# Last convolution's output: GpSimd rounds image 0 in place, VectorE goes on with the sum of image 1

## The chip, the cores and the metric

The kernel runs on one core of one Trainium2 chip. The metric is the device time of one execution in microseconds, as the median of several runs. A core has TensorE (matmul, results in PSUM), VectorE, ScalarE and GpSimd for elementwise work, and SyncE, which here only starts transfers. The engines run side by side, each through its own list of instructions in order, and wait for one another by semaphores. GpSimd's work in this kernel reads and writes SBUF only.

## The reference, cut to what matters

The input is 4 images of 64 channels, 32 x 32 pixels. Four blocks follow each other: a spatial attention (L0), two 3x3 convolutions with quantised weights and batch norms (L1), two 3x3 convolutions with 4-bit weights and activations (L2), and a box convolution with batch norms (L3). The change is in the output of block L2:

```
def qfn(x, k):
    n = float(2 ** k - 1)
    return ste_round(x * n) / n

def act_quant(x, k):
    return qfn(jnp.clip(x, 0.0, 1.0), k)
...
out = act_quant(bn_eval(conv3x3(x, wq1), gamma1, beta1, mean1, var1), A_BIT)
wq2 = weight_quant(w2, W_BIT) * mask
out = bn_eval(conv3x3(out, wq2), gamma2, beta2, mean2, var2)
out = out + x
return act_quant(out, A_BIT)
```

Block L3 then takes this output in two ways: as the input of a 1x1 convolution to 16 channels (with a batch norm over all images and a relu), and as the residual of its own output.

## The kernel before

The kernel is written engine by engine: one Python function for each (`sp`, `pe`, `act`, `dve`, `pool`) lists its instructions in the order in which it runs them, with explicit waits (`wait_ge`) and signals (`then_inc`). No scheduler moves anything. All data stay in SBUF; an image is a tile of 128 partitions (64 channels, twice) by 512 elements.

The stage of the change is the end of L2. TensorE convolves the four images of the last convolution (`main_taps` and `side_taps3`, lines 476 and 507) into four PSUM banks, images 0 and 1 first, then 2, then 3. For each image VectorE's `outer(b)` adds the scaled convolution and `x15`, which is the block's input times 15 with the bias added, that GpSimd made earlier (L1328), into `tmpo` (the sum, L1119). It then adds a large constant, which rounds to an integer, and takes the minimum (L1122, in place in `tmpo`). ScalarE's `outer_clip(b)` subtracts the constant, clips at zero and writes the integers as bf16 into `xi` (ScalarE's lines all show as L685, its helper `run`). Image 3 has no clip on ScalarE: VectorE does it with two instructions (L1124, L1126), the second of which waits until ScalarE's clips of images 0 to 2 are signalled.

Within VectorE the helper `link` makes an instruction signal the semaphore `chain` and then waits for it, so that the next instruction finds the result written. The rounding therefore waits for the sum, while the sum of the next image doesn't wait for the rounding.

TensorE takes `xi` in this order: `spread(0)`, `spread(1)` (L614, for the residual), `bottleneck(0, 1, 2)` (L605, the 1x1 convolution of three images side by side in three groups of columns), `spread(2)`, `bottleneck(3)`, `spread(3)`. ScalarE copies each spread image from PSUM (`x_out`), after its three clips. VectorE, after image 3, transposes the first half of image 0's copy (`residual_out`, L1153) and takes the statistics of the bottleneck's result (`bn_stats` into `hst`, L1158), which waits for `bottleneck(3)`. From there single instructions on VectorE, TensorE and ScalarE make scale and shift, and the box convolution, the last batch norm, the relu and the stores follow. GpSimd does nothing between `x15` and the final sums (`pool_sums`, L1335 and L1337). Other lines that matter below: `add_residual` (L1103), the same form as the sum L1119, `low_part` (L903), VectorE's differences of `rows_w` (L1139) and GpSimd's clip of the edges (L1296).

Of the kernel before, what the change touches and what calls it, by code (L numbers as in the profile page):

```python
# [24 lines left out]
ALU = mybir.AluOpType  # L25
# [12 lines left out]
MAGIC = 12582912.0  # L38
QN, QP = -4.0, 3.0
LEVELS = 15.0  # L40
# [24 lines left out]
BANKS = ((6, 4, 5, 0), (7, 1, 2, 3))  # L65
# [25 lines left out]
def build(nc, x, wa, wg_raw, wconv, par, cst, out):  # L91
# [3 lines left out]
    for n, (kind, _) in enumerate(uses):  # L95
        by_act.append((by_act[-1] if by_act else 0) + (kind != "D"))
        by_dve.append((by_dve[-1] if by_dve else 0) + (kind == "D"))
# [3 lines left out]
    with ExitStack() as ctx:  # L101
        def sb(name, shape, dt=F32):
            return ctx.enter_context(nc.sbuf_tensor(name, [128] + shape, dt))

        def sem(name):
            return ctx.enter_context(nc.semaphore(name))
# [33 lines left out]
        ev_scale = sb("ev_scale", [2])  # L140
# [54 lines left out]
        tmpo = sb("tmpo", [NB, HALF])  # L195
        x15 = sb("x15", [NB, HALF])
# [7 lines left out]
        ps = ctx.enter_context(nc.psum_tensor("ps", [128, 8, 512], F32))  # L204
# [21 lines left out]
        def flat(t):  # L226
            return t.rearrange("q o n -> q (o n)")
# [23 lines left out]
        def split_count(k, b):  # L251
# [12 lines left out]
        sum_ready = sem("sum_ready")  # L264
        q_relu, q_int, q_ready = sem("q_relu"), sem("q_int"), sem("q_ready")
        x15_ready, xi_ready, xi_up = sem("x15_ready"), sem("xi_ready"), sem("xi_up")
        h_raw, h_stat, h_all, h_var, h_sqrt, h_ab, h_ready = (sem(n) for n in (
            "h_raw", "h_stat", "h_all", "h_var", "h_sqrt", "h_ab", "h_ready"))
        hblk_ready = sem("hblk_ready")
# [411 lines left out]
        def _(act):  # L681
            act.dma_start(wbc[:], wa[:, 0:256 + HEAD]).then_inc(wa_in, 16)

            def run(o, i, f, **kw):
                return nc.scalar.activation(o, i, f, **kw)  # L685
# [32 lines left out]
            for kind, i in uses:  # L718
                if kind != "S":
                    continue  # L720
                b, t = divmod(i, JT)
# [41 lines left out]

            def outer_clip(b):

                act.wait_ge(xi_up, b + 1)
                run(xi[:, b, :], tmpo[:, b, :], ACT.Relu, bias=consts[:, K_MAGIC:K_MAGIC + 1]).then_inc(xi_ready, 1)

            for b in range(NB):
# [3 lines left out]
            for b in range(NB - 1):  # L773
                outer_clip(b)
# [59 lines left out]
        def _(dve):  # L834
            V = nc.vector
            links = [0]

            def link(ins):

                links[0] += 1  # L840
                ins.then_inc(chain, 1)
                dve.wait_ge(chain, links[0])
# [155 lines left out]
            for kind, i in uses:  # L998
# [4 lines left out]
                b, t = divmod(i, JT)  # L1003
# [110 lines left out]
            def outer(b):  # L1114

                v = tmpo[:, b, :]
                dve.wait_ge(conv_done[3], b + 1)
                dve.wait_ge(x15_ready, b + 1)
                link(V.scalar_tensor_tensor(v, ps[:, BANKS[1][b], :], ev_scale[:, 1:2], x15[:, b, :],  # L1119
                                            ALU.mult, ALU.add))  # L1120
                if b < NB - 1:
                    V.tensor_scalar(v, v, MAGIC, MAGIC + LEVELS, ALU.add, ALU.min).then_inc(xi_up, 1)  # L1122
                    return
                link(V.tensor_scalar(xi[:, b, :], v, MAGIC, MAGIC, ALU.add, ALU.subtract))  # L1124
                dve.wait_ge(xi_ready, b)
                V.tensor_scalar(xi[:, b, :], xi[:, b, :], 0.0, LEVELS, ALU.max, ALU.min).then_inc(xi_ready, 1)  # L1126
# [17 lines left out]
            for b in range(NB):  # L1144
                outer(b)
# [114 lines left out]
        @block.gpsimd  # L1260
        def _(pool):
            G = nc.gpsimd
            links = [0]


            def link(ins):

                links[0] += 1
                ins.then_inc(pchain, 1)
                pool.wait_ge(pchain, links[0])  # L1270

            G.memset(wq[:].bitcast(F32), 0.0).then_inc(wq_zero, 1)
            G.memset(w2[:].bitcast(F32), 0.0).then_inc(wq_zero, 1)
            G.memset(w3[:], 0.0).then_inc(wq_zero, 1)
            pool.wait_ge(wq_zero, 3)
            pool.wait_ge(cst_in, 16)
            G.tensor_copy(ident_bf[:], consts[:, K_ID:K_ID + 128]).then_inc(id_ready, 1)
            pool.wait_ge(id_ready, 1)

            def pieces(t):  # L1280

                n = C * W // PIECES
                return [t[:, n * p:n * (p + 1)] for p in range(PIECES)]

            def edge(i, offset, table):


                n = C // PIECES
                for p in range(PIECES):
                    G.tensor_tensor(edge_buf[i][:, n * W * p:n * W * (p + 1)].rearrange("q (k j) -> q k j", j=W),  # L1290
                                    parm[:, offset + n * p:offset + n * (p + 1)].unsqueeze(2).to_broadcast([128, n, W]),
                                    consts[:, table:table + W].unsqueeze(1).to_broadcast([128, n, W]), ALU.add)\
                        .then_inc(edge_sum, 1)
                pool.wait_ge(edge_sum, PIECES * (i + 1))
                for v in pieces(edge_buf[i]):
                    G.tensor_scalar(v, v, 1.0, 0.0, ALU.min, ALU.max).then_inc(edge_clip, 1)  # L1296

            pool.wait_ge(par_in, 16)
            w1 = parm[:, P_W1:P_W1 + OC]
            link(G.memset(wp[:], 0.0))  # L1300
            link(G.tensor_copy(w1p[:, 0, :], w1))
            link(G.tensor_tensor(w1f[:], w1, w1p[:, 0, :], ALU.subtract))
            link(G.tensor_copy(w1p[:, 1, :], w1f[:]))
            link(G.tensor_tensor(w1p[:, 2, :], w1f[:], w1p[:, 1, :], ALU.subtract))
            link(G.tensor_copy(wp[0:64, :, 0:OC], w1p[0:64]))
            G.tensor_copy(wp[64:128, :, OC:2 * OC], w1p[64:128]).then_inc(wp_ready, 1)
            pool.wait_ge(wp_ready, 1)

            edge(0, P_XMAX, K_IR1)
            edge(1, P_XMIN, K_IR)  # L1310
            edge(2, P_YMAX, K_JW1)
            edge(3, P_YMIN, K_JW)

            pool.wait_ge(wmax_part, 2)
            G.partition_all_reduce(wmax_all[:], wmax[:], 128, bass.bass_isa.ReduceOp.max).then_inc(wmax_done, 1)
            pool.wait_ge(wmax_done, 1)
            G.memset(img3[:], 0.0).then_inc(img3_zero, 1)
            pool.wait_ge(img3_zero, 1)

            pool.wait_ge(lo_done, NB)  # L1320
            pool.wait_ge(edge_clip, 4 * PIECES)
            for hi, lo in zip(pieces(edge_buf[2]), pieces(edge_buf[3])):
                G.tensor_tensor(lo, hi, lo, ALU.subtract).then_inc(cols_ready, 1)  # L1323

            pool.wait_ge(ev_ready, 1)
            for b in range(NB):
                pool.wait_ge(gen[2], b + 1)
                G.tensor_scalar(x15[:, b, :], y3[:, b, :], LEVELS, ev_bias[:, 1:2], ALU.mult, ALU.add)\  # L1328
                    .then_inc(x15_ready, 1)

            def pool_sums(i):

                two = slice(SUM_POOL[2 * i], SUM_POOL[2 * i] + 2)
                pool.wait_ge(f_lin, 2 * i + 2)
                G.tensor_tensor(flat(fo[:, two, :]), flat(fo[:, two, :]), flat(xf[:, two, :]), ALU.add).then_inc(f_sum, 1)  # L1335
                pool.wait_ge(f_sum, i + 1)
                G.tensor_scalar(flat(fo[:, two, :]), flat(fo[:, two, :]), 0.0, None, ALU.max).then_inc(f_out_pool, 1)  # L1337

            pool.wait_ge(xf_ready, 2 * NB)
            for i in range(len(SUM_POOL) // 2):  # L1340
                pool_sums(i)
# [88 lines left out]
```

## Time and profile before

| what | value |
|---|---|
| median of 3 runs | 157.21 us (157.13 to 157.22) |
| the profiled execution | 158.21 us |
| its span | 156.4 us |
| TensorE matmul, busy share of the span | 90% |
| VectorE | 75% |
| ScalarE | 54% |
| GpSimd | 33% |
| mean granted TensorE clock | 0.98 |

The profiled execution is a run of its own: its time is 1.00 us above the median of the others, and 1.81 us of it lie outside the span. Busy shares are averages over stages with different limits. In rows of a timeline the first number is the start in us from the span's start, the second the time covered; "x3" with one time is three instructions that overlap or follow each other. A bracket tells how long the engine was idle before it and what ended that.

### The profile page before, as it was taken

To read this page: it belongs to the slowest core of one execution; us is meant where nothing else is said; L and a number is where in the kernel's file an instruction comes from. 1 tells how busy PE (TensorE), PEld (TensorE's weight loads), DVE (VectorE), ACT (ScalarE), POOL (GpSimd) and SP (SyncE) were. 2 spreads that over 40 slices of the span, in tenths; PEclk is the share of its full clock that TensorE was granted. 3 is DMA by queue.
4 is the path that set the end of the run, shared out by engine and by line. 5 is a ranking of instruction groups with operands and counts; after the bars stand their busy time and mean duration, and the time that the engine had idled before them with its cause. 6 is when DMAs were issued, how large, how long until landed. Compare 5 with 4: busy or idle time off the path is not lost.

```text
span 156.4 us, 2621 instructions
## 1 busy us (share of the span) xinstructions
PE 140.5 (90%) x945; PEld 65.9 (42%) x945; DVE 117.5 (75%) x280; ACT 83.8 (54%) x138; POOL 51.6 (33%) x97
## 2 busy tenths in 40 slices
PE   7989999999999999999999997999979996989600
PEld 2244422333323432333345854786357632378500
DVE  2189989899878789999912667787788569875882
ACT  3135566356766777467815105995192537533282
POOL 7018999999910006000000950000066000000080
PEclk9999999999999999999999999999999999999975
DMA  3586020200002000000000000001000000000015
GB/s 101 133 293 272 4 66 3 67 2 0 0 6 67 0 0 0 0 0 4 0 0 0 0 0 2 4 0 38 0 0 0 4 0 0 0 6 4 0 67 201
DMA packets 2748, 5.27 MB, mean 34 GB/s; under 512 B 368, under 2 KB 1200, under 8 KB 2608
## 3 DMA queue, kind: packets, MB, share of 16 engines
q1 hardware_dynamic: 2592, 4.98, 10.3%
q8 instruction: 7, 0.11, 0.3%
q10 hardware_dynamic: 144, 0.13, 0.3%
q14 instruction: 5, 0.04, 0.1%
HBM read 3.13 MB, written 1.05 MB: 27 GB/s over the span
## 4 chain that ended last, share of the span: by engine, by line
PE 69%; DVE 15%; ACT 6%; issue 5%; DMA 2%; ACTq 0%; DVEq 0%
PE ps L420 16%; PE ps L412 15%; PE ps L476 13%; PE ps L493 7%; DVE nmax L1006 3%; PE ps L490 3%; PE ps L352 3%; PE ps L639 3%; DMA wbc<-wa 2%; ACT box_t L685 2%; DVE dz L896 2%; PE ps L648 2%; DVE tmpo L1119 1%; PE ps L380 1%; PE ps L362 1%
## 5 line engine op out<-in xcount | busy, mean ns | idle before, releaser
L685 ACT ACTIVATE probs<-ps,nmax 128x1024 f32<-128x1024 f32 x32 | 35.6, 1114 | 25.9 <-DVE nmax L1006 25.9
L1006 DVE TENSOR_REDUCE nmax<-ps 128x1 f32<-128x1024 f32 x32 | 39.0, 1220 | 4.8 <-PE ps L412 4.5
L420 PE MATMUL ps<-probs,dz 128*64 128x512 f32 x128 | 31.4, 606 | 0.0
L412 PE MATMUL ps<-xd,g 64*128 64x512 f32 x48 | 24.0, 616 | 0.4 <-ACT probs L685 0.4
L412 PE MATMUL ps<-xd,g_other 64*128 64x512 f32 x48 | 24.0, 616 | 0.0
L420 PEld LDWEIGHTS ps<-probs,dz 128*64 128x64 f32 x128 | 7.6, 136 | 20.6 <-issue 16.9
L476 PE MATMUL ps<-img,wq 128*128 128x512 f32 x48 | 13.6, 422 | 1.0 <-ACT img L685 0.8
L1323 POOL TENSOR_TENSOR box_t<-box_t 128x256 f32<-128x256 f32 x8 | 6.1, 797 | 24.1 <-issue 24.1
L1290 POOL TENSOR_TENSOR box_t<-parm,consts 128x256 f32<-128x256 f32 x24 | 13.9, 617 | 0.0
L903 DVE TENSOR_TENSOR img<-y,img 128x512 fp32r<-128x512 f32 x11 | 7.6, 690 | 8.1 <-ACT y L685 8.1
L896 DVE TENSOR_SCALAR dz<-d,rz 128x64 f32<-128x64 f32 x32 | 12.2, 381 | 1.1
L1328 POOL TENSOR_SCALAR x<-y,ev_bias 128x512 f32<-128x512 f32 x4 | 5.1, 1274 | 23.0 <-ACT y L685 22.7
L490 PE MATMUL ps<-img,wq 64*128 64x512 f32 x48 | 12.3, 408 | 0.0
L493 PE MATMUL ps<-img,wq 64*128 64x512 f32 x48 | 12.2, 407 | 0.0
L476 PEld LDWEIGHTS ps<-img,wq 128*128 128x128 f32 x48 | 8.5, 189 | 7.5 <-issue 3.7
L412 PEld LDWEIGHTS ps<-xd,g_other 64*128 64x128 f32 x48 | 7.9, 186 | 7.7 <-ACT probs L685 3.5
L1335 POOL TENSOR_TENSOR box_t<-box_t 128x256 f32<-128x256 f32 x2 | 1.4, 724 | 28.6 <-ACT box_t L685 28.6
L412 PEld LDWEIGHTS ps<-xd,g 64*128 64x128 f32 x48 | 7.9, 186 | 6.9 <-issue 4.9
L547 PE MATMUL ps<-spin,ident_bf 128*128 128x512 bf16 x41 | 9.9, 380 | 0.0
L493 PEld LDWEIGHTS ps<-img,wq 64*128 64x128 f32 x48 | 8.8, 187 | 1.8
L476 PE MATMUL ps<-img,w 128*128 128x512 f32 (+1 forms) x30 | 8.2, 416 | 1.3 <-ACT img L685 0.9
L490 PEld LDWEIGHTS ps<-img,wq 64*128 64x128 f32 x48 | 8.7, 185 | 0.9 <-issue 0.8
(177 smaller groups left out, 242.7 us busy)
## 6 DMA issues: line engine op xcount, KB each, us to landing
wraw<-wconv SPq DMA_DIRECT2D x1, 1152.0 KB, 7.8
xd<-x SPq DMA_DIRECT2D x4, 256.0 KB, 4.7
g_other<-g SPq DMA_DIRECT2D x6, 128.0 KB, 2.3
out<-box_t SPq DMA_DIRECT2D x3, 256.0 KB, 2.5
consts<-cst SPq DMA_DIRECT2D x1, 327.0 KB, 4.2
out<-box_t SPq DMA_DIRECT2D x2, 128.0 KB, 2.2
wdd<-wa SPq DMA_DIRECT2D x1, 192.0 KB, 2.4
parm<-par SPq DMA_DIRECT2D x1, 163.0 KB, 2.5
```

What stands on the lines that cost most here:

```text
L412: last = mm(o[:, 512 * p:512 * p + 512], rows, cols, start=True, stop=True)
L420: last = mm(y[64 * p:64 * p + 64, :], dz[:, g % DZ, :], probs[:, g % PROBS, 512 * p:512 * p + 512], start=g == 0, stop=t == JT - 1)
L476: last = mm(ps[:, BANKS[k % 2][b], :], main_weights(k, b, kh), image(part, b, kh) if k < 3 else image3(b, kh), start=begin and part == kh ...
L490: o = mm(ps[:, BANKS[k % 2][odd], :], side_weights(k, odd, slice(64, 128), a), image(part, odd, a + down, -1, slice(64, 128)), start=begin ...
L493: e = mm(ps[:, BANKS[k % 2][even], :], side_weights(k, even, slice(0, 64), a), image(part, even, a, 1, slice(0, 64)), start=False, stop=en ...
L547: mm(ps[:, bank, :], ident_bf[:], spin[:], start=True, stop=True)
L685: return nc.scalar.activation(o, i, f, **kw)
L896: V.tensor_scalar(dz[:, g % DZ, :], d32[:, b % 2, t, :], rz[:, g:g + 1], None, ALU.mult)\
L903: V.tensor_tensor(image(1, b), as_rows(y_of[k][:, b, :]), image(0, b).bitcast(F32), ALU.subtract)\
L1006: V.tensor_reduce(nmax[:, i:i + 1], slot(("S", i)), AX.X, ALU.min).then_inc(max_ready, 1)
L1290: G.tensor_tensor(edge_buf[i][:, n * W * p:n * W * (p + 1)].rearrange("q (k j) -> q k j", j=W), parm[:, offset + n * p:offset + n * (p + 1 ...
L1323: G.tensor_tensor(lo, hi, lo, ALU.subtract).then_inc(cols_ready, 1)
```

## The change

Image 0's rounding moves from VectorE to GpSimd. VectorE's `outer(0)` now ends with the sum, which signals `outer_sum` and is not waited for on VectorE. GpSimd waits for that signal and does the same instruction (add, minimum) in place in `tmpo`, with a signal `xi_up_pool`. ScalarE's clip of image 0 waits for this new signal, and the clips of images 1 and 2 for a count that is lower by one. Images 1 to 3 are treated as before.

```diff
+        outer_sum, xi_up_pool = sem("outer_sum"), sem("xi_up_pool")
...
             def outer_clip(b):
 
-                act.wait_ge(xi_up, b + 1)
+                if b == 0:
+                    act.wait_ge(xi_up_pool, 1)
+                else:
+                    act.wait_ge(xi_up, b)
                 run(xi[:, b, :], tmpo[:, b, :], ACT.Relu, bias=consts[:, K_MAGIC:K_MAGIC + 1]).then_inc(xi_ready, 1)
...
                 dve.wait_ge(x15_ready, b + 1)
-                link(V.scalar_tensor_tensor(v, ps[:, BANKS[1][b], :], ev_scale[:, 1:2], x15[:, b, :],
-                                            ALU.mult, ALU.add))
+                total = V.scalar_tensor_tensor(v, ps[:, BANKS[1][b], :], ev_scale[:, 1:2], x15[:, b, :],
+                                               ALU.mult, ALU.add)
+                if b == 0:
+                    total.then_inc(outer_sum, 1)
+                    return
+                link(total)
                 if b < NB - 1:
                     V.tensor_scalar(v, v, MAGIC, MAGIC + LEVELS, ALU.add, ALU.min).then_inc(xi_up, 1)
                     return
...
+            pool.wait_ge(outer_sum, 1)
+            G.tensor_scalar(tmpo[:, 0, :], tmpo[:, 0, :], MAGIC, MAGIC + LEVELS, ALU.add, ALU.min).then_inc(xi_up_pool, 1)
+
             def pool_sums(i):
```

## Rows read from the trace of the kernel before

**Rows 1.** the page of the profile, its first line (core 0 alone)

```profile
span 156.4 us, 2621 instructions
```

**Rows 2.** the chain that ended last: start us, us, what ran

```profile
126.74 0.64 PE ps L507 x8
...
130.85 0.73 ACT xi L685
```

**Rows 3.** timeline of VectorE, outer() and after it: start us, us, instruction

```profile
127.36 0.75 DVE L1119 SCALAR_TENSOR_TENSOR tmpo<-ps,ev_scale,x 128x512 f32<-128x512 f32 x1 [0.40 <-PE ps L507]
...
128.15 0.43 DVE L1122 TENSOR_SCALAR tmpo<-tmpo 128x512 f32<-128x512 f32 x1
...
128.49 0.74 DVE L1119 SCALAR_TENSOR_TENSOR tmpo<-ps,ev_scale,x 128x512 f32<-128x512 f32 x1
...
130.39 0.43 DVE L1122 TENSOR_SCALAR tmpo<-tmpo 128x512 f32<-128x512 f32 x1
...
130.73 0.74 DVE L1119 SCALAR_TENSOR_TENSOR tmpo<-ps,ev_scale,x 128x512 f32<-128x512 f32 x1
...
131.51 0.43 DVE L1124 TENSOR_SCALAR xi<-tmpo 128x512 bf16<-128x512 f32 x1
...
131.97 0.29 DVE L1126 TENSOR_SCALAR xi<-xi 128x512 bf16<-128x512 bf16 x1
...
132.18 0.64 DVE L1153 STREAM_TRANSPOSE box_t<-y 128x256 f32<-128x256 f32 x1
...
133.18 0.70 DVE L1158 BATCH_NORM_STATS2 hst<-ps 128x6 f32<-128x512 f32 x1 [0.36 <-PE ps L605]
```

**Rows 4.** timeline of ScalarE, the clips and the first copies behind them

```profile
128.61 0.72 ACT L685 ACTIVATE xi<-tmpo,consts 128x512 bf16<-128x512 f32 x1 [2.45 <-DVE tmpo L1122]
...
130.85 0.72 ACT L685 ACTIVATE xi<-tmpo,consts 128x512 bf16<-128x512 f32 x1 [0.40 <-DVE tmpo L1122]
...
131.48 0.58 ACT L685 ACTIVATE y<-ps 128x512 f32<-128x512 f32 x1
```

**Rows 5.** timeline of TensorE, last convolution and its readers

```profile
128.31 0.39 PE L507 MATMUL ps<-img,w3x 64*64 64x512 bf16 x1
...
128.63 0.86 PE L476 MATMUL ps<-img,w3x 128*128 128x512 bf16 x3
...
131.63 0.40 PE L605 MATMUL ps<-xi,wp 128*32 128x512 bf16 x3 [0.71 <-ACT xi L685]
...
132.29 0.39 PE L614 MATMUL ps<-xi,ident_bf 128*32 128x512 bf16 x3
...
132.32 0.39 PE L605 MATMUL ps<-xi,wp 128*32 128x512 bf16 x1
```

**Rows 6.** timeline of GpSimd's one-input work and VectorE and ScalarE beside it

```profile
112.34 2.07 DVE L1103 SCALAR_TENSOR_TENSOR tmp<-ps,bn_a,y 128x512 f32<-128x512 f32 x3
...
113.84 0.71 ACT L685 ACTIVATE y<-tmp,bn_b 128x512 f32<-128x512 f32 x1
...
114.65 0.69 DVE L903 TENSOR_TENSOR img<-y,img 128x512 fp32r<-128x512 f32 x1 [0.24 <-ACT y L685]
...
114.73 1.18 POOL L1328 TENSOR_SCALAR x<-y,ev_bias 128x512 f32<-128x512 f32 x1 [22.72 <-ACT y L685]
...
115.26 0.74 DVE L1103 SCALAR_TENSOR_TENSOR tmp<-ps,bn_a,y 128x512 f32<-128x512 f32 x1
```

**Rows 7.** timeline, GpSimd's fourth of these and VectorE beside it

```profile
118.46 1.65 POOL L1328 TENSOR_SCALAR x<-y,ev_bias 128x512 f32<-128x512 f32 x1
...
118.94 0.68 DVE L1139 TENSOR_TENSOR rows_w<-rows_w,box_t 128x512 f32<-128x512 f32 x1
...
119.54 1.10 DVE L1139 TENSOR_TENSOR rows_w<-rows_w,box_t 128x512 f32<-128x512 f32 x1
```

**Rows 8.** groups of GpSimd by line and shape: xcount, busy us, mean ns

```profile
L1296 POOL TENSOR_SCALAR box_t<-box_t 128x256 f32<-128x256 f32 x24 | 8.8, 400 | 0.3
...
L1337 POOL TENSOR_SCALAR box_t<-box_t 128x256 f32<-128x256 f32 x2 | 1.7, 867 | 0.2
```

## The prediction

> **What bounds the kernel now.** I read the page first: one core, a span of 156.4 us [rows 1], VectorE and TensorE shared between many short stages, so the share of busy time decides nothing here. The chain that ended last tells where the changed stage lies on it [rows 2]: it runs from the last convolution's matmuls (L507) into VectorE's `outer`, and from there over ScalarE's clip of image 2 into TensorE. The whole stage is on the path. The timeline of VectorE then gives its rhythm [rows 3]. Image 0's sum (L1119) starts at 127.36 and takes 0.75; the rounding (L1122) may only start when the sum's result is there, at 128.15; image 1's sum starts at 128.49. So one image costs 1.13 us, the fourth sum starts at 130.73, its two roundings (L1124, L1126) end at 131.94 and 132.26, and bn_stats of the bottleneck starts at 133.18, released by TensorE's L605. In between lies TensorE's bottleneck matmul of image 3 [rows 5]: its first one starts at 132.32, 0.06 after image 3's integers are written (132.26). The matmuls of images 0 to 2 and the spread of image 2 start at 131.63 and 132.29; so image 3's matmul comes both 0.06 behind VectorE and 0.69 behind the start of that row of matmuls, and I have to move both.
>
> TensorE is not what holds the sums. Image 1 is convolved with image 0 (the chain's L507 row ends at 127.38 for both [rows 2]), image 2 is complete at 128.31 + 0.39 = 128.70, image 3 at 128.63 + 0.86 = 129.49 [rows 5], and each is earlier than its sum would start even after the change (below).
>
> **The change, part by part.** *Removed from VectorE:* the rounding of image 0 (0.43 us) and the wait for the sum ahead of it. Two of these sums without a wait between them can be seen in the residual sums, the same form at L1103: three in 2.07 us, so (2.07 - 0.74)/2 = 0.665 us from start to start [rows 6]. Image 1's sum would then start at 127.36 + 0.665 = 128.03 in place of 128.49: 0.46 us earlier. With the same steps as before, all behind it moves by 0.46: image 1's rounding starts at 128.81 and ends at 129.24, image 2's sum starts at 129.15 (its convolution is done at 128.70), image 2's rounding starts at 129.93, image 3's sum at 130.27 (done at 129.49), and image 3's integers are ready at 131.80.
>
> *Added on GpSimd:* one tensor_scalar 128x512 f32 in place. GpSimd is idle there; its fourth x15 has ended by 120.11 [rows 7], and behind the new instruction its queue holds only the sums of the final stage, so nothing waits there. Its start: ScalarE's y ended at 113.84 + 0.71 = 114.55 and GpSimd's x15, which had waited for it, started at 114.73 [rows 6], so I take 0.18 from a foreign engine's end to GpSimd's start: 128.11 + 0.18 = 128.29. Its duration is the open number. The nearest shape is x15 itself (L1328), which shows 1.18 us [rows 6], but a VectorE instruction with two tensors in SBUF (L903) ran from 114.65 to 115.34 beside it, and 114.73 + 1.18 - 115.34 leaves 0.57. The fourth x15 [rows 7] took 1.65 and says the same from the other side: if it could begin only when VectorE's first L1139 ended or gave way (119.54), 0.57 is left until 120.11; and the L1139 instruction of 119.54 took 1.10 in place of its neighbour's 0.68, ending 0.53 behind GpSimd. So the two engines exclude one another in such instructions, and x15 alone is about 0.57, with what start-up was hidden under the wait on top. The two-operation clip at half the size takes 0.40 [rows 8], which makes 0.80 at most for twice the elements. I take 0.65, between 0.57 and 0.80. The new instruction also has two operations (add, min), like those two. GpSimd then ends at 128.94 (128.86 to 129.09).
>
> *Does it collide with VectorE?* While it runs, VectorE does image 1's sum (128.03 to 128.77), one input in PSUM and one in SBUF. The same form, L1103 at 115.26, took its usual 0.74 while x15 did its 0.57 of work beside it [rows 6]: no collision. Image 1's rounding at 128.81 is an SBUF to SBUF instruction with one tensor, and I must assume that it is shut out until GpSimd is done. In the pair of rows 7 the shut-out instruction ended 0.53 behind GpSimd with 0.68 of its own, so 0.15 of it was already behind it; then the rounding ends at 128.94 + 0.43 - 0.15 = 129.22, not later than the 129.24 above. With 0.80 it would be 129.37, a loss of 0.13.
>
> [...]
>
> *ScalarE and its waits.* The clip of image 0 waited for VectorE until 128.61 [rows 4]; now it waits for GpSimd. No row has that step; between 0.04 (a sum's end to the instruction that waits for it, 128.11 to 128.15) and the 0.18 above, I take 0.10: it starts at 129.04, 0.43 later than before. Behind it in ScalarE's queue are the clips of images 1 and 2 and then the copies for the residual. ScalarE's instructions follow each other every 0.63 us (130.85 to 131.48 [rows 4]), so clip 2 could start at 129.04 + 1.26 = 130.30, before its own input at 130.85 - 0.46 = 130.39. Thus the later clip 0 is caught up, with 0.09 to spare; clip 2 is 0.46 earlier, and TensorE's row of bottleneck matmuls starts at 131.17. Image 3's matmul then starts at 131.17 + 0.69 = 131.86, and by VectorE's integers at 131.80 + 0.06 = 131.86: both 0.46 earlier than 132.32. The last rounding also waits for clip 2, which ends at 130.39 + 0.72 = 131.11, before it needs it. The transpose behind it (132.18, now 131.72) needs ScalarE's first copy, at 131.48 + 0.58 - 0.46 = 131.60. The count that clips 1 and 2 wait for is lowered with the signals, and costs nothing. GpSimd's own wait for the sum's signal delays nobody, as the final sums behind it need the boxes that are computed later.
>
> *Behind the stage* the order of work is unchanged and each step waits for another of the same group, down to the stores; no step there waits for something that stays where it is. So the whole shift arrives: 0.46. The profiled execution took 158.21 with 156.4 of span, 1.81 outside it; it would be 157.75 with a span of 155.94. It lies 1.00 above the median of 157.21, and the same shift gives **156.75 us** there, 0.29% less.
>
> **The rivals.**
>
> *(A) GpSimd's instruction is as long as x15 shows, 1.18 us, exclusion or not.* For it: that is what the record says [rows 6]. Against: the fourth record is 1.65 [rows 7], and the two differ just as their VectorE neighbours do. It would end at 129.47, image 1's rounding at 129.75, 0.51 late: no gain is left, 157.26. The gain is gone from about 1.13 us on.
>
> [...]
>
> *(C) The other side: a slow form on GpSimd.* Its relu (L1337, one operation and none behind it) takes 0.87 for 256 elements a partition [rows 8], where the clip takes 0.40. If add and min went that way, it would be between 0.87 and 1.73, by an estimate 1.5 (twice 0.87 less one start-up of some 0.2). GpSimd would end at 129.79, VectorE's rounding of image 1 at 130.07, 0.83 behind plan, so 0.83 - 0.46 = 0.37 slower than before: 157.58; at 1.73 it is 157.81. It is slower by over 0.2% from about 1.45 us on. Against it: both nearest forms with two operations are fast.
>
> *(D) The gain is made but part of it is swallowed*: a start of GpSimd beyond 0.18 after its 8 us of idleness, 0.80 us of duration, or a clip 0 that comes later; each eats one for one once the 0.02 and 0.09 of slack are gone. Some 0.2 lost gives 156.95.
>
> **How the numbers follow.** About 0.2%, 0.31 us, is what a measurement of this kernel can tell from none. Chances: the forecast 0.60; A 0.10, B 0.06 and D 0.12 fall within 0.2% of before (D at 156.95 is just inside); C 0.12. That makes faster 0.60, same 0.28, slower 0.12. The likeliest case alone has 156.62 to 156.90 (0.13 from the duration's upper end, as much below for what start-to-start times may hold). The range reaches from there through D, A and B towards C: 156.60 to 157.45.
>
> **What would show it.** In the changed profile: L1119's second instance starting some 0.67 behind the first; a GpSimd row of 0.57 to 0.80 beside it; image 1's rounding not longer than 0.6; ScalarE's clip 0 about 0.4 later, clip 2 0.46 earlier; bn_stats at 132.72 and the span near 155.9. [...] If bn_stats is 0.46 earlier and the span is not shorter, my reading of what follows the stage is wrong.

## The result and the profile after

The changed kernel takes 158.21 us (median of 6 runs, 157.87 to 158.61) against 157.17 us of the kernel before in the same comparison (6 runs, 156.94 to 157.32): ratio 1.0073, 95% interval 1.0046 to 1.0101. It is slower by about 1.1 us, where 0.46 us less was forecast, and lies outside the range. The profiled execution took 158.47 us with a span of 156.3.

That span is as long as the one of before [rows 1], and yet the kernel is slower: in the two profiled executions image 0's sum starts at different times, 127.36 before and 126.02 after. Everything up to there is the same program, and that start wanders from one execution to another (125.6 to 126.8 in most of the profiles below). So I compare two distances from this start: to `bn_stats` of the bottleneck (the stage), and to the end of the span (the tail). Before they are 133.18 - 127.36 = 5.82 and 156.4 - 127.36 = 29.04 us [rows 1, 3]; after, 6.86 and 30.28. The tail is 1.24 us longer; that is the loss as these two executions show it, beside 1.04 us between the medians. (Spans are given to 0.1 us, so a tail is good to about 0.05.) The kernel before also runs inside the experiment `bench` below, and there its stage is 131.38 - 125.57 = 5.81. In the later comparisons some executions, the profiled one of `pair` among them, ran in a second state that is over 1.5% slower, and the ratios leave them out.

VectorE's timeline after, the rows that answer to [rows 3] (line numbers have moved on: L1123 is the sum, L1130 the rounding, L1134 image 3's last instruction, L1166 bn_stats):

```profile
126.02 1.41 DVE L1123 SCALAR_TENSOR_TENSOR tmpo<-ps,ev_scale,x 128x512 f32<-128x512 f32 x2 [0.41 <-PE ps L508]
127.47 0.43 DVE L1130 TENSOR_SCALAR tmpo<-tmpo 128x512 f32<-128x512 f32 x1
...
128.59 0.53 DVE L1130 TENSOR_SCALAR tmpo<-tmpo 128x512 f32<-128x512 f32 x1
...
130.93 0.29 DVE L1134 TENSOR_SCALAR xi<-xi 128x512 bf16<-128x512 bf16 x1 [0.69 <-ACT xi L686]
...
132.88 0.70 DVE L1166 BATCH_NORM_STATS2 hst<-ps 128x6 f32<-128x512 f32 x1 [0.84 <-PE ps L606]
```

VectorE does what was forecast: two sums in 1.41 us, the second 0.66 behind the first. Image 1's rounding starts at 127.47 and takes its usual 0.43. Image 2's takes 0.53. But image 3's last instruction, free to start at 130.24, waits 0.69 us for ScalarE, and bn_stats waits for TensorE. GpSimd's new instruction, and the three clips on ScalarE:

```profile
126.86 1.98 POOL L1340 TENSOR_SCALAR tmpo<-tmpo 128x512 f32<-128x512 f32 x1 [8.07 <-DVE tmpo L1123]
...
128.88 1.95 ACT L686 ACTIVATE xi<-tmpo,consts 128x512 bf16<-128x512 f32 x3 [4.06 <-POOL tmpo L1340]
```

GpSimd takes 1.98 us, not 0.65. The clips run one behind another from 128.88 to 130.83, which is 4.81 us behind the sum's start; before, the third ended at 131.57, 4.21 behind it [rows 4]. The chain that ended last goes over GpSimd's instruction, the clips of images 0 and 1 and then TensorE, with the second image's spread (L615) ahead of the bottleneck (L606):

```profile
126.86 1.99 POOL tmpo L1340
...
128.88 1.34 ACT xi L686 x2
...
130.26 0.62 PE ps L615 x3
130.89 0.60 PE ps L606 x3
...
131.53 0.85 PE ps L606 x8
```

TensorE's timeline in the same stretch, answering to [rows 5] (L615 spreads, L606 bottleneck):

```profile
127.29 0.86 PE L477 MATMUL ps<-img,w3x 128*128 128x512 bf16 x3
129.74 1.14 PE L615 MATMUL ps<-xi,ident_bf 128*32 128x512 bf16 x8 [1.59 <-ACT xi L686]
130.88 0.61 PE L606 MATMUL ps<-xi,wp 128*32 128x512 bf16 x3
...
131.28 1.11 PE L606 MATMUL ps<-xi,wp 128*32 128x512 bf16 x8
```

Its last convolution ends at 128.15 and the eight spread matmuls start late, at 129.74. The first four of them still take 0.41 us; from 130.26 on, where the chain has its L615 row, each matmul takes 0.6. The table by windows shows why (us, busy of PE, PEld, DVE, ACT, POOL, then the granted clock as a share of full speed):

```profile
core 0: us, PE busy (x) PEld busy (x) DVE busy (x) ACT busy (x) POOL busy (x), PEclk, DMA share, GB/s
128.00:129.00 1.00, 0.15 (x1) 0.00 (x0) 0.97 (x2) 0.12 (x1) 0.84 (x1) 1.00 0.00 0
129.00:130.00 1.00, 0.26 (x4) 0.15 (x4) 0.96 (x3) 1.00 (x2) 0.00 (x0) 1.00 0.00 0
130.00:131.00 1.00, 0.89 (x12) 0.24 (x11) 0.31 (x2) 1.00 (x3) 0.00 (x0) 0.66 0.00 0
131.00:132.00 1.00, 1.00 (x12) 0.43 (x13) 0.81 (x2) 0.79 (x2) 0.00 (x0) 0.50 0.00 0
132.00:133.00 1.00, 1.00 (x12) 0.20 (x4) 0.16 (x2) 0.17 (x1) 0.00 (x0) 0.50 0.00 0
```

The granted clock falls from 1.00 to 0.50 after TensorE was busy for only 0.15 and 0.26 of two microseconds. Before, TensorE had a thin stretch too, and kept 1.00; its spread matmuls of image 0 followed the last convolution at once, and it stood for 0.61 and 0.71 us ahead of the two groups of matmuls behind them:

```profile
129.36:130.36 1.00, 0.53 (x5) 0.15 (x4) 1.00 (x2) 0.63 (x1) 0.00 (x0) 1.00 0.00 0
130.36:131.36 1.00, 0.41 (x4) 0.12 (x4) 0.97 (x2) 0.60 (x2) 0.00 (x0) 1.00 0.00 0
131.36:132.36 1.00, 0.73 (x14) 0.41 (x18) 0.93 (x4) 1.00 (x3) 0.00 (x0) 1.00 0.00 0
```

So two things are new: a long GpSimd instruction and a low clock. The experiments take them apart.

### The profile page after: what moved, and what is told of

Same layout as the page of the kernel before. It is cut to its first block, busy times and chain, and to the rows that moved or that the text cites. A ratio compares the mean times of both kernels' runs of the same rounds, so it can differ in the third digit from the quotient of the medians.

```text
span 156.3 us, 2621 instructions
## 1 busy us (share of the span) xinstructions
PE 139.8 (89%) x945; PEld 65.6 (42%) x945; DVE 116.2 (74%) x279; ACT 83.5 (53%) x138; POOL 54.1 (35%) x98
## 4 chain that ended last, share of the span: by engine, by line
PE 73%; DVE 12%; ACT 6%; issue 3%; DMA 3%; POOL 1%; ACTq 0%; DVEq 0%
PE ps L421 18%; PE ps L413 17%; PE ps L477 13%; PE ps L494 5%; PE ps L491 5%; DMA wbc<-wa 3%; PE ps L353 3%; PE ps L640 3%; DVE nmax L1010 2%; ACT box_t L686 2%; PE ps L649 2%; PE ps L381 1%; POOL tmpo L1340 1%; PE ps L548 1%; DVE st L1196 1%
## 5 line engine op out<-in xcount | busy, mean ns | idle before, releaser
L1331 POOL TENSOR_TENSOR box_t<-box_t 128x256 f32<-128x256 f32 x8 | 6.1, 796 | 24.1 <-issue 24.1
L900 DVE TENSOR_SCALAR dz<-d,rz 128x64 f32<-128x64 f32 x32 | 10.8, 337 | 1.1
L1304 POOL TENSOR_SCALAR box_t<-box_t 128x256 f32<-128x256 f32 x24 | 9.3, 419 | 0.3
```

The lines of the kernel that those rows point to most:

```text
L900: V.tensor_scalar(dz[:, g % DZ, :], d32[:, b % 2, t, :], rz[:, g:g + 1], None, ALU.mult)\
```

## The experiments

All stages and tails, from one profiled execution each, with the time ratio to the kernel before where it was timed:

| kernel | stage us | tail us | ratio (95% interval) |
|---|---|---|---|
| before | 5.82 | 29.04 | |
| before, in bench | 5.81 | | |
| changed | 6.86 | 30.28 | 1.0073 (1.0046 to 1.0101) |
| changed, again | 6.85 | 30.38 | 1.0072 (1.0038 to 1.0107) |
| warm | 6.11 | 29.27 | 1.0014 (0.9987 to 1.0041) |
| min_add | 6.83 | 30.46 | 1.0070 (1.0042 to 1.0099) |
| no_round | 5.36 | 28.58 | 0.9948 (0.9924 to 0.9972) |
| mult_add | 5.35 | 28.59 | 0.9977 (0.9945 to 1.0010) |
| pair | 5.65 | 28.85 | 0.9977 (0.9945 to 1.0009) |
| reorder | 5.51 | 28.75 | 0.9976 (0.9948 to 1.0003) |
| reorder, again | 5.50 | 28.64 | 0.9959 (0.9926 to 0.9992) |
| reorder_fill | 5.67 | 28.76 | 0.9978 (0.9949 to 1.0006) |
| reorder_pair | 5.37 | 28.56 | 0.9951 (0.9918 to 0.9985) |

Single runs of one kernel spread by over 1 us here, so a ratio tells less than a tail; where the two are named together, the tail is the finer measure of the stage and the ratio the check on it.

**bench: what one GpSimd instruction costs.** To the kernel before, behind its last relu:

```diff
+            link(G.tensor_scalar(s0, s0, M, M + LEVELS, ALU.add, ALU.min))
...
+            link(G.tensor_scalar(s0, s0, LEVELS, M, ALU.min, ALU.add))
+            link(G.tensor_scalar(s0, s0, 1.0, 1.5, ALU.mult, ALU.add))
+            link(G.tensor_scalar(s0, s0, LEVELS, ev_bias[:, 1:2], ALU.mult, ALU.add))
+            link(G.tensor_scalar(s0, s0, 1.0, 0.0, ALU.min, ALU.max))
+            link(G.tensor_scalar(s0, s0, 1.5, 0.0, ALU.add, ALU.max))
+            link(G.tensor_scalar(s0, s0, 1.5, None, ALU.add))
+            link(G.tensor_scalar(s0, s0, 0.0, None, ALU.max))
+            link(G.tensor_scalar(s0, s0, 1.5, LEVELS, ALU.add, ALU.min))
...
+            link(G.tensor_scalar(s1, s0, M, M + LEVELS, ALU.add, ALU.min))
```

> The kernel before, and behind its last relu a series of GpSimd tensor_scalar instructions on a spare tile while VectorE is idle, each waited for, then four meetings of one GpSimd instruction with a row of VectorE instructions. The meetings are in f32 128x512: (add, min) beside sums from PSUM and SBUF, (add, min) beside in-place SBUF tensor_scalars, then (min, max) beside the same two. The added work computes nothing of the output. Theory 1, the pair of operations sets the time: (add, min) takes 1.7 to 2.0 us alone, while (min, max) and (mult, add) take 0.57 to 0.80. Theory 2, VectorE slows it: (add, min) alone takes 0.57 to 0.80 and gets to some 2 us only in the meetings. Theory 3, the large constant or the in-place form sets it: then (add, min) with 1.5 and 15, or into another tile, is the short one.

GpSimd's timeline, VectorE idle. L1367 is (add, min) with the large constant, L1369 (min, add), L1370 (mult, add), L1371 (mult, add) with a per-partition operand, L1372 (min, max), L1374 add alone, L1375 max alone, L1376 (add, min) with small numbers, L1379 (add, min) into another tile:

```profile
151.97 1.95 POOL L1367 TENSOR_SCALAR scr<-scr 128x512 f32<-128x512 f32 x1 [0.66 <-DVE box_t L1233]
...
156.00 1.93 POOL L1369 TENSOR_SCALAR scr<-scr 128x512 f32<-128x512 f32 x1
158.01 0.62 POOL L1370 TENSOR_SCALAR scr<-scr 128x512 f32<-128x512 f32 x1
158.73 0.69 POOL L1371 TENSOR_SCALAR scr<-scr,ev_bias 128x512 f32<-128x512 f32 x1
159.50 0.61 POOL L1372 TENSOR_SCALAR scr<-scr 128x512 f32<-128x512 f32 x1
...
162.21 1.50 POOL L1374 TENSOR_SCALAR scr<-scr 128x512 f32<-128x512 f32 x1
163.79 1.49 POOL L1375 TENSOR_SCALAR scr<-scr 128x512 f32<-128x512 f32 x1
165.36 1.93 POOL L1376 TENSOR_SCALAR scr<-scr 128x512 f32<-128x512 f32 x1
...
169.00 1.92 POOL L1379 TENSOR_SCALAR scr<-scr 128x512 f32<-128x512 f32 x1
```

Theory 1 holds for the forms of this series: the operations, singly or in pairs, go with the time. (mult, add) and (min, max) take 0.61 to 0.69 us, every other form tried 1.49 to 1.95, on the same 128x512 f32 tile. (add, max) took 1.93 as well. Small numbers (L1376, 1.93) and another tile (L1379, 1.92) change nothing. The four meetings, (add, min) beside sums and beside SBUF roundings, then (min, max) beside the same:

```profile
173.14 1.92 POOL L1383 TENSOR_SCALAR scr<-scr 128x512 f32<-128x512 f32 x1 [0.94 <-DVE scd L1273]
176.74 2.15 POOL L1385 TENSOR_SCALAR scr<-scr 128x512 f32<-128x512 f32 x1 [1.69 <-DVE scd L1268]
180.97 0.61 POOL L1387 TENSOR_SCALAR scr<-scr 128x512 f32<-128x512 f32 x1 [2.08 <-DVE scd L1273]
184.57 0.85 POOL L1389 TENSOR_SCALAR scr<-scr 128x512 f32<-128x512 f32 x1 [2.99 <-DVE scd L1268]
```

Beside sums from PSUM the instruction is as long as alone (1.92, 0.61); beside roundings it is 0.22 to 0.24 longer. On VectorE, of the roundings that met the slow instruction two were long, the rest 0.43:

```profile
177.16 0.71 DVE L1271 TENSOR_SCALAR scd<-scd 128x512 f32<-128x512 f32 x1
...
178.36 0.81 DVE L1271 TENSOR_SCALAR scd<-scd 128x512 f32<-128x512 f32 x1
```

**min_add: the other order of operations.**

```diff
-            G.tensor_scalar(tmpo[:, 0, :], tmpo[:, 0, :], MAGIC, MAGIC + LEVELS, ALU.add, ALU.min)
+            G.tensor_scalar(tmpo[:, 0, :], tmpo[:, 0, :], LEVELS, MAGIC, ALU.min, ALU.add)
```

> The changed kernel with GpSimd's two operations in the other order: minimum with 15 first, then plus the constant (the same result). If (add, min) in this order is what is slow, the GpSimd record falls from 1.98 to 0.6 to 0.8 us and the time to the 156.75 us that was forecast, or some 0.1 above it. If any add on GpSimd is slow, or if VectorE beside it makes it slow, the record stays at 1.7 to 2.0 us and the time at 158.2.

The record is 1.96 us and the ratio 1.0070: no remedy, in agreement with L1369.

**no_round: VectorE's part of the change alone.** Left out are the rounding and the upper clip of image 0.

```diff
-                    act.wait_ge(xi_up_pool, 1)
+                    act.wait_ge(outer_sum, 1)
...
-                run(xi[:, b, :], tmpo[:, b, :], ACT.Relu, bias=consts[:, K_MAGIC:K_MAGIC + 1]).then_inc(xi_ready, 1)
+                run(xi[:, b, :], tmpo[:, b, :], ACT.Relu, bias=0.0 if b == 0 else consts[:, K_MAGIC:K_MAGIC + 1])\
+                    .then_inc(xi_ready, 1)
...
-            pool.wait_ge(outer_sum, 1)
-            G.tensor_scalar(tmpo[:, 0, :], tmpo[:, 0, :], MAGIC, MAGIC + LEVELS, ALU.add, ALU.min).then_inc(xi_up_pool, 1)
```

> The changed kernel without any rounding of image 0: GpSimd does nothing there and ScalarE's clip of image 0 waits for VectorE's sum (left out: the rounding and the upper clip of image 0). My first account of VectorE's part: each later sum starts 0.46 us earlier and all of it arrives at the end, 156.7 us. If TensorE or ScalarE's chain takes it up, bn_stats starts less than 0.46 us earlier behind the start of image 0's sum (before: 5.82 us) and the time is 156.9 to 157.2.

```profile
126.62 1.41 DVE L1124 SCALAR_TENSOR_TENSOR tmpo<-ps,ev_scale,x 128x512 f32<-128x512 f32 x2 [0.40 <-PE ps L508]
...
130.78 0.29 DVE L1135 TENSOR_SCALAR xi<-xi 128x512 bf16<-128x512 bf16 x1
...
131.98 0.70 DVE L1167 BATCH_NORM_STATS2 hst<-ps 128x6 f32<-128x512 f32 x1 [0.37 <-PE ps L606]
```

The stage is 131.98 - 126.62 = 5.36 us and the tail 28.58: 0.46 less than before in both, the forecast number. The ratio, 0.8 us less with 0.4 to 1.2 as its interval, agrees with it. So the forecast of VectorE's gain, and that all of it arrives at the end, was right.

**mult_add: the change with a fast pair.** Left out is the upper clip of image 0.

```diff
-            G.tensor_scalar(tmpo[:, 0, :], tmpo[:, 0, :], MAGIC, MAGIC + LEVELS, ALU.add, ALU.min)
+            G.tensor_scalar(tmpo[:, 0, :], tmpo[:, 0, :], 1.0, MAGIC, ALU.mult, ALU.add)
```

> The changed kernel with GpSimd's pair of operations set to (mult by 1, add constant), which rounds but leaves out the upper clip of image 0. By the series of single instructions it takes 0.62 us. If the length of this one instruction is the whole of what my forecast missed, bn_stats comes 5.36 us behind the start of image 0's sum (0.46 less than before), the clock stays at 1.00 and the time is 156.75 us, ratio about 0.997. If the two engines' exclusion costs more than the sum allowed for (a rounding on VectorE that waits for GpSimd), it is 5.4 to 5.7 us and 156.8 to 157.1.

```profile
127.55 0.62 POOL L1340 TENSOR_SCALAR tmpo<-tmpo 128x512 f32<-128x512 f32 x1 [8.10 <-DVE tmpo L1123]
...
128.15 0.43 DVE L1130 TENSOR_SCALAR tmpo<-tmpo 128x512 f32<-128x512 f32 x1
...
132.06 0.70 DVE L1166 BATCH_NORM_STATS2 hst<-ps 128x6 f32<-128x512 f32 x1 [0.35 <-PE ps L606]
```

GpSimd takes 0.62, image 1's rounding starts as it ends and takes 0.43, and the stage is 132.06 - 126.71 = 5.35. With a duration near the 0.65 that the forecast took, the stage is the forecast one (5.36) to 0.01 us. GpSimd started 0.09 us after the sum's end (126.71 + 0.75 = 127.46) and not 0.18, so the meeting with image 1's rounding that the forecast allowed for hardly took place, and this run doesn't test that part of the sum. The ratio, 0.9977, has the right side but its interval just includes 1.

**warm: TensorE kept busy while it waits for image 0.**

```diff
+            keep_busy(9, BANKS[0][3])
             spread(0)
             spread(1)
             bottleneck(0, 1, 2)
```

> The changed kernel with nine filler matmuls on TensorE ahead of the first spread, to cover its wait for image 0. If the granted clock of 0.5 between 130.7 and 133.4 us is a cost of its own that comes from TensorE's idle time ahead of it, the clock stays at 1.00 there, bn_stats starts 0.45 us earlier behind the start of image 0's sum (6.4 us in place of 6.86) and the time is 157.6 to 157.8 us, against 158.2 of the changed kernel and 157.2 before. If GpSimd's long rounding alone makes the loss, the fillers change nothing: 158.2 us.

The same windows as above:

```profile
130.00:131.00 1.00, 1.00 (x9) 0.31 (x6) 0.97 (x2) 1.00 (x3) 0.00 (x0) 1.00 0.00 0
131.00:132.00 1.00, 0.80 (x15) 0.36 (x14) 0.31 (x2) 1.00 (x3) 0.00 (x0) 1.00 0.00 0
132.00:133.00 1.00, 1.00 (x20) 0.42 (x13) 0.73 (x3) 0.81 (x3) 0.00 (x0) 1.00 0.00 0
```

and bn_stats:

```profile
132.94 0.70 DVE L1167 BATCH_NORM_STATS2 hst<-ps 128x6 f32<-128x512 f32 x1
```

GpSimd still takes 1.98 us, and clip 2 ends as late behind the sum's start (4.80 us) as in the changed kernel (4.81). The first spread starts even later than there, 4.00 us behind the sum's start in place of 3.72, since the fillers run until about 130.8. But the clock stays at 1.00, from clip 2's end to bn_stats it takes 1.31 us in place of 2.05, and the stage is 132.94 - 126.83 = 6.11 in place of 6.86: in these profiles 0.75 us of the loss were the clock. In the times, the ratio goes from the 1.0070 of `min_add`, in the same comparison, to 1.0014. What is left, 0.29 us of stage and 0.23 of tail, is the length of the GpSimd instruction, less what the change gains on VectorE. It is less than I expected (a stage of 6.4), because image 3's integers are ready at 132.02, only 0.34 behind the start of the row of bottleneck matmuls; before they were ready 0.63 behind it:

```profile
131.68 0.40 PE L606 MATMUL ps<-xi,wp 128*32 128x512 bf16 x3 [0.20 <-ACT xi L687]
...
131.73 0.29 DVE L1135 TENSOR_SCALAR xi<-xi 128x512 bf16<-128x512 bf16 x1 [0.69 <-ACT xi L687]
```

**pair, reorder, reorder_fill, reorder_pair: versions that keep the result.** `pair` uses two fast pairs:

```diff
-            G.tensor_scalar(tmpo[:, 0, :], tmpo[:, 0, :], MAGIC, MAGIC + LEVELS, ALU.add, ALU.min).then_inc(xi_up_pool, 1)
+            link(G.tensor_scalar(tmpo[:, 0, :], tmpo[:, 0, :], LEVELS, 0.0, ALU.min, ALU.max))
+            G.tensor_scalar(tmpo[:, 0, :], tmpo[:, 0, :], 1.0, MAGIC, ALU.mult, ALU.add).then_inc(xi_up_pool, 1)
```

> The changed kernel with GpSimd's one slow instruction replaced by two of the fast pairs: (min 15, max 0), then (mult 1, add constant), the same result after the clip. Each takes 0.62 us alone; the second one meets VectorE's rounding of image 1 and waits for it, so that both end some 1.7 us after the sum in place of 2.1. ScalarE's clip 0 then starts 0.4 us earlier than in the changed kernel, TensorE's idle time is shorter, and if the clock stays at 1.00 bn_stats comes 5.7 to 5.9 us behind the start of image 0's sum and the time is that of before, ratio 0.999 to 1.001. If the clock falls again, 6.4 us or more and ratio over 1.003.

`reorder` leaves the slow instruction and asks for image 0 later (the counts that the spreads and ScalarE's copies wait for are set to match; `reorder_fill` has fillers of 4 and 3 matmuls ahead of its two first spreads as well):

```diff
-            for b in range(NB - 1):
+            for b in (1, 0, 2):
                 outer_clip(b)
...
+            spread(1)
             spread(0)
-            spread(1)
-            bottleneck(0, 1, 2)
+            bottleneck(0, 1)
             spread(2)
-            bottleneck(3).then_inc(h_raw, 1)
+            bottleneck(2, 3).then_inc(h_raw, 1)
```

> The changed kernel with another order behind the roundings: ScalarE clips image 1, 0, 2; TensorE spreads 1, then 0, then runs the bottleneck of images 0 and 1, spreads 2, and runs the bottleneck of 2 and 3 side by side. GpSimd's 1.98 us then end 2.8 us behind the start of image 0's sum, where clip 0 is wanted at 2.6. If length and order are what matter, bn_stats comes at 5.4 us behind that start and the time is 156.8 us; if TensorE's idle time still lowers its clock, at 6.0 us or later and 157.4 us or more.

> The same with four filler matmuls ahead of the first spread and three ahead of the second. With the clock held, bn_stats at 5.4 us behind the start of image 0's sum, 156.8 us (0.3% under before), whatever the one without fillers does; if fillers hold up the spreads, 0.1 us more.

> The other order with the one slow instruction once more, beside the other two: bn_stats at 5.51 us behind the start of image 0's sum, 0.31 less than before, ratio 0.998, that is between no difference and 0.3% less.

`reorder_pair` is both:

> The two fast pairs together with the other order (ScalarE clips 1, 0, 2; bottleneck of images 0 and 1, then of 2 and 3). GpSimd's part is done before clip 1 has left ScalarE, and no rounding on VectorE meets it late, so bn_stats comes at 5.41 us behind the start of image 0's sum, 0.10 less than with the slow instruction, and the time is 0.25% under before. If VectorE's rounding of image 1 loses more by the meeting than the rounding of image 2 did (0.10 us), it is 5.5 to 5.7 us.

In `reorder`, image 2's rounding meets the end of GpSimd's instruction and takes 0.53, and bn_stats comes 131.36 - 125.85 = 5.51 behind the sum's start, 0.31 less than before but 0.1 more than the 5.4 that I expected. Its repetition has 5.50 and, unlike the first, a ratio whose interval lies below 1:

```profile
128.42 0.53 DVE L1130 TENSOR_SCALAR tmpo<-tmpo 128x512 f32<-128x512 f32 x1
...
131.36 0.70 DVE L1166 BATCH_NORM_STATS2 hst<-ps 128x6 f32<-128x512 f32 x1
```

The fillers of `reorder_fill` bought nothing: the clock was at 1.00 without them, and they held up the second spread; its stage is 5.67 (forecast 5.4), its tail the same. `pair` has a stage of 5.65, just below the forecast 5.7 to 5.9, and its second instruction took 0.81. The stage started late in its profile, at 128.55, which the distances leave out. `reorder_pair` is the shortest:

```profile
125.84 1.41 DVE L1123 SCALAR_TENSOR_TENSOR tmpo<-ps,ev_scale,x 128x512 f32<-128x512 f32 x2 [0.40 <-PE ps L508]
...
131.21 0.70 DVE L1166 BATCH_NORM_STATS2 hst<-ps 128x6 f32<-128x512 f32 x1 [0.27 <-PE ps L606]
```

```profile
126.69 0.61 POOL L1340 TENSOR_SCALAR tmpo<-tmpo 128x512 f32<-128x512 f32 x1 [8.11 <-DVE tmpo L1123]
127.38 0.81 POOL L1341 TENSOR_SCALAR tmpo<-tmpo 128x512 f32<-128x512 f32 x1
```

No rounding is lengthened (0.43 each), and the stage is 131.21 - 125.84 = 5.37, as good as with no rounding of image 0 at all (5.36, in the old order). Its median is 156.68 us beside 157.50 of the kernel before in its comparison, ratio 0.9951 (0.9918 to 0.9985): it beats the kernel before, by more than the 0.25% that I expected, and with that the changed one. Between it and `reorder` (0.9959 in the same comparison) the times can't tell; the tails differ by 0.08 to 0.19 us, where the two profiles of `reorder` itself differ by 0.11.

**after_again: the changed kernel once more.**

> The changed kernel itself, for comparison on the same chip: 158.2 us, ratio 1.007; bn_stats 6.86 us behind the start of image 0's sum and a granted clock of 0.5 in between, if that is a property of the kernel; if the low clock came and went from one execution to another, this profile would show it at 1.00.

Stage 6.85, granted clock 0.50 from 131 to 134 us, ratio 1.0072. The low clock was in all three profiles that start the spreads so late without fillers (changed, changed again, min_add). The mean clock over the whole span is 0.964 to 0.975 in all six executions of the first comparison, but in `after_again` and `min_add` some have 0.979 to 0.981, as the kernel before has. (Its mean is not 1.00 because every profile shows 0.50 from some 148 to 151 us to the end, behind TensorE's last matmul, where it has nothing left to run; a fall of 3 us in the stage takes off another 0.01.) So it is likely that those executions don't have the fall, or not all of it. If it costs 0.75 us, they should be that much shorter. In `after_again` they are: 157.86 us, the median of five, against 158.57 of four with the low mean. In `min_add` they are not: 158.38 of three against 158.18 of six. And both groups stay 0.8 us or more above the kernel before (157.05 and 157.24). What the fall costs in single executions is thus open; the 0.75 is what the profiles show.

## Why the prediction was wrong

**The step that failed** is the duration of the added instruction: "I take 0.65, between 0.57 and 0.80. The new instruction also has two operations (add, min), like those two." The number of operations didn't decide it: in `bench` one operation took 1.49 and 1.50 us, two took from 0.61 to 1.95. The two rows that I leaned on, x15 (mult, add) and the edge clip (min, max), are the two pairs that were fast there (0.62 or 0.69, and 0.61 us); (add, min) took 1.98 us. The row that told of it was on the table: the relu, 0.87 us at half the size against 0.40 of the clip [rows 8]. I read its slowness as belonging to one operation, and gave that case (C) 0.12. The upper end was too low even there: twice 0.87 is 1.73, and in the series (add, max) took some 0.4 more than add alone (1.93 against 1.50). The forecast stage was 5.36 us behind the sum's start and the measured one 6.86; with GpSimd at its 1.98 us and the clock held it was 6.11 (`warm`), so this step by itself accounts for 0.75 of the 1.50 us; the rest is the clock, which its lateness brought down (below).

**Rival C had the right cause and the wrong path.** It let VectorE wait for GpSimd: image 1's rounding 0.83 late. On the chip that rounding ran its 0.43 us in the middle of GpSimd's 1.98. The forecast's sum shuts it out until GpSimd's end as well; that was my assumption for an instruction with one tensor, and no run shows it. The delay went through ScalarE instead: clip 0 started 2.86 us behind the sum's start, the clips of 1 and 2 could only follow at 0.63 each, and clip 2 ended 0.60 later than before. The forecast had this queue in it, with 0.09 us to spare, but case C didn't ask what it costs.

**What no case had is TensorE's clock,** a term that the forecast put at nothing. I followed only the last-ending waits. Clip 0 started 2.86 us behind the sum's start in place of 1.25 [rows 3, 4], so the first spread came only at 129.74, after 1.59 us in which TensorE stood still. The forecast had no wait for that spread on its path, yet TensorE's idle time ahead of it cost 0.75 of the 1.04 us of stage by the profiles: `warm` gives these back with the clock, though its spread starts later still. The forecast did notice that clip 0 would be late and called it caught up; what it did not ask is what TensorE does meanwhile. After 1.59 us with nothing to run its clock fell to 0.50 (from 130.3 us on); with fillers in that gap it stayed at 1.00 (`warm`).

**What held.** VectorE's gain of 0.46 us and its arrival at the end (no_round). No collision of GpSimd with sums from PSUM (1.92 alone and beside them). The place of VectorE's first rounding behind a 0.6 us instruction (mult_add), though there by an earlier start of GpSimd and not by the slack that the forecast reckoned with. With a duration near the one taken, the forecast of 0.46 less is met: 5.35 against 5.36. x15's own length was read nearly rightly from its neighbours, 0.57 out of 1.18: alone, that form takes 0.69. So rival A's reason was wrong. That GpSimd and VectorE exclude one another where VectorE has two tensors in SBUF stays my reading of [rows 6, 7]; no experiment took it apart. The chance of 0.06 under B was for a GpSimd that starts only at the end of image 1's sum; in mult_add it started beside that sum, 0.09 us behind the end of image 0's.

**Sum of the loss**, in distances behind the sum's start: GpSimd's long instruction costs 0.75 (6.11 against 5.36), VectorE's gain takes 0.46 off it, which leaves 0.29, and with 0.75 from the clock that makes 1.04 us of stage; behind bn_stats the changed kernel's tail is 0.20 longer still (23.42 against 23.22), and with the clock held it is not (23.16), so this too goes to the clock. Together 1.24. The three profiles with the low clock have 23.42 to 23.63 us there, all the others 23.09 to 23.24. The share of the clock is that of profiled executions; see `after_again` for what the times leave open.

## What to carry to other kernels

Before work is moved to GpSimd, find a row with the same pair of operations; the same instruction name and shape are not enough (0.61 to 1.95 us for one name and one shape here), and a row of the same engine that is twice as long as another of its size (0.87 against 0.40 us here) is a warning. Where a result is handed to a slower engine, move also the order in which it is asked for: the same slow instruction that cost 1.1 us with image 0 asked for first gained 0.3 to 0.4 us by the tails with image 0 asked for second. And when an early, harmless-looking consumer on TensorE comes later, look at how long TensorE then stands still, and price the clock: here 1.59 us of standing came with a clock of 0.50 and 0.75 us of the stage, 1.12 us (`pair`) with a clock of 1.00.

## What the runs showed of the hardware

- GpSimd's tensor_scalar on 128x512 f32: 0.61 (min, max), 0.62 (mult, add), 0.69 (mult, add with a per-partition operand), 1.49 (max) and 1.50 (add), 1.92 to 1.95 (add, min), (min, add) and (add, max). On 128x256: 0.40 (min, max), 1.06 (add, min). From 256 to 512 elements a partition (min, max) grew by 0.21 us and (add, min) by 0.86.
- GpSimd's slow (add, min) did not shut VectorE out for its whole length: in the changed kernel a rounding ran its usual 0.43 us in the middle of GpSimd's 1.98, where the shut-out that the prediction assumed would have held it for 1.4 us (127.47 to 128.84). The next one took 0.53, and in `bench` two took 0.71 and 0.81. With the fast pairs the roundings that met GpSimd took up to 0.72, and GpSimd's second instruction in `pair` and `reorder_pair` 0.81, where its form took 0.62 alone.
- In the changed kernel TensorE's granted clock fell from 1.00 to 0.50 for some 3 us from about 130.3 us on, after TensorE had stood from 128.15 to 129.74 and been busy for 0.15 and 0.26 of two microseconds. It didn't fall in the kernel before, which stood for 0.61 and 0.71 us (busy 0.53 and 0.41), nor in `pair`, which stood for 1.12 us ahead of its first spread. With fillers in the gap (`warm`) it didn't fall either.
